# An expert's first product computed transposed, in a fused mixture-of-experts and FFN kernel

## The reference

```
tid = clip(token_ids, 0, 24999);  e = min(tid // 6250, 3)
g = silu(xn @ M.T);  u = xn @ M.T;  y = (g * u) @ M.T      # einsum 'bsd,fd', M = ctx[e]
x = x + tanh(g_xattn) * y
h2 = layernorm(x)
f = silu(h2 @ Wg * gate_scale) * (h2 @ Wu * up_scale)      # weights rounded to fp8, 512 -> 1536
x = x + tanh(g_ffn) * (f @ Wd) * down_scale                # 1536 -> 512
```

## Time and profile before

| | |
|---|---|
| median of 3 runs | 424.04 us (422.85 to 427.6) |
| the profiled execution's own time | 427.73 us |
| its span | 426.0 us |
| PE busy, and matmuls | 395.8 us (93%), x2010 |
| DVE, ACT, POOL busy | 234.5, 183.2, 168.9 us |
| steps 0 to 18, from the first Z matmul to the end of Z of step 18 | 23.0 to 156.7 us |

### The profile page before, as it was taken

How to read it: one execution, slowest core, us unless ns; L and a number is a source line. 1 busy time by engine, 2 the same in 40 slices (tenths; PEclk the granted TensorE clock), 3 DMA queues, 4 the chain that set the end, 5 groups by cost and what they waited for, 6 DMA issues and landing times.

```text
span 426.0 us, 6383 instructions
## 1 busy us (share of the span) xinstructions
PE 395.8 (93%) x2010; PEld 197.9 (46%) x2010; DVE 234.5 (55%) x503; ACT 183.2 (43%) x298; POOL 168.9 (40%) x190
## 2 busy tenths in 40 slices
PE   3959799999999999899999999999999999999991
PEld 2625445555555555444444444444444444444440
DVE  5676778988988678477642422224322225222244
ACT  4484547677786654865352222222222222222220
POOL 2437167764586658799630800001700002600003
PEclk9997989999999999999999999999999999999996
DMA  7575212211113101222000100000200000200002
GB/s 277 160 257 151 72 27 76 74 32 46 49 52 75 49 28 51 74 79 93 2 2 2 74 26 0 0 2 0 98 0 0 0 0 0 100 0 0 2 1 98
DMA packets 10508, 22.66 MB, mean 53 GB/s; under 512 B 1624, under 2 KB 1648, under 8 KB 10480
## 3 DMA queue, kind: packets, MB, share of 16 engines
q1 hardware_dynamic: 7920, 13.92, 10.5%
q0 software_dynamic: 2560, 8.39, 6.0%
HBM read 18.11 MB, written 4.19 MB: 52 GB/s over the span
## 4 chain that ended last, share of the span: by engine, by line
PE 84%; DVE 6%; POOL 4%; issue 2%; DMA 1%; ACT 1%; DVEq 0%; POOLq 0%; ACTq 0%
PE bank L1281 35%; PE bank L1194 24%; PE bank L1289 17%; PE bank L1126 5%; POOL w_sum L470 2%; POOL W L473 2%; PE bank L1148 1%; DVE Ml L794 1%; PE bank L1180 1%; DMA xs<-in_x,order 1%; DVE row_hot L777 1%; DVE w_big L836 1%; DVE xs L1107 1%; DMA ws<-in_L_ffn_down_w 1%; DVE X L1104 1%
## 5 line engine op out<-in xcount | busy, mean ns | idle before, releaser
L1281 PE MATMUL bank<-X,W 128*128 128x512 f16 (+1 forms) x768 | 173.5, 379 | 1.0 <-DVE late_norms L1046 1.0
L1281 PEld LDWEIGHTS bank<-X,W 128*128 128x128 bf16 x768 | 74.9, 98 | 92.0 <-DVE late_norms L1046 2.5
L1057 DVE SCALAR_TENSOR_TENSOR cs<-bank,up_mul,cs 128x512 f32<-128x512 f32 x48 | 36.0, 749 | 107.7 <-PE bank L1281 106.2
L1289 PE MATMUL bank<-W,cs 128*128 128x512 bf16 x376 | 88.7, 379 | 1.6 <-DVE X L856 1.6
L645 ACT ACTIVATE cs<-bank,gate_mul 128x512 f32<-128x512 f32 x48 | 32.9, 685 | 76.6 <-PE bank L1281 76.6
L506 POOL TENSOR_TENSOR xs<-xs,X 128x512 f32<-128x512 f32 x12 | 15.3, 1272 | 121.3 <-DVE X L1104 121.0
L652 ACT ACTIVATE cs<-cs 128x512 f16<-128x512 f32 x47 | 29.5, 628 | 76.0 <-DVE cs L1057 76.0
L1194 PE MATMUL bank<-Mh,X 128*128 x152 | 51.4, 401 | 8.6 <-DVE Ml L794 6.1
L1289 PEld LDWEIGHTS bank<-W,cs 128*128 128x128 f16 x376 | 36.5, 98 | 45.2 <-issue 1.8
L1065 DVE TENSOR_TENSOR cs<-cs 128x512 f16<-128x512 f32 x47 | 35.3, 751 | 37.1 <-ACT cs L652 36.0
L470 POOL TENSOR_TENSOR w_sum<-ws,w_big 128x512 f32<-128x512 f32 x36 | 47.3, 1313 | 5.1 <-DVE w_big L836 2.7
(11 more groups left out here) (145 smaller groups left out, 413.8 us busy)
## 6 DMA issues: line engine op xcount, KB each, us to landing
ws<-in_L_ffn_gate_w SPq DMA_DIRECT2D x12, 256.0 KB, 2.8
ws<-in_L_ffn_up_w SPq DMA_DIRECT2D x12, 256.0 KB, 2.6
ws<-in_L_ffn_down_w SPq DMA_DIRECT2D x12, 256.0 KB, 2.5
cs<-in_ctx SPq DMA_DIRECT2D x2, 1024.0 KB, 6.5
X<-in_ctx SPq DMA_DIRECT2D x2, 1024.0 KB, 7.0
xs<-in_x,order POOLq DMA_INDIRECT x16, 3.6
dsc<-in_L_ffn_down_scale SPq DMA_DIRECT2D x1, 256.0 KB, 7.3
out<-xs,order POOLq DMA_INDIRECT x16, 2.8
```

The lines of the kernel that those rows point to most:

```text
L1057: v.scalar_tensor_tensor(out=fuse[:, c % 2, :], in0=UP[c % 2][:], scalar=up_mul[:, c:c + 1], in1=sg[:, c % 2, :], op0=ALU.mult, op1=ALU.mu ...
L1281: ins = t_.matmul(dst[c % 2][:].rearrange("p (t i) -> p t i", t=TPG), w, x2_group(g, part, k), start=(k == 0 and part == 0), stop=(k == KC ...
L1289: ins = t_.matmul(ACC[t][:], fuse_part(g, c, part)[:, t * P:(t + 1) * P], W8[:, down_slab(c), :], start=(c == 0 and part == 0), stop=(c == ...
```

## The change

Z is computed transposed. For each of four column blocks f of the matrix, and each of four k, a 128 x 128 block of the matrix stands still and the 128 columns of the x tile stream: 48 matmuls of 128 x 128 in place of 12 of 128 x 512. Z then comes out with h's index on the partitions, so h needs no transposes: `turn_h`, bank `HT` and `hT_done` go, and `hTh`, `hTl` are made from `h` in SBUF. The scales of a step, picked by a register before, are read from step 4 on at a fixed column of three small tables, which VectorE fills once at the end of step 3.

```diff
-                    act.wait_ge(hT_done, s)
+                    act.wait_ge(h_done, s)
...
-                    a.activation(hTh[:], HT[:], ACT.Copy).then_inc(hhi_done, 1)
+                    a.activation(hTh[:], h[:], ACT.Copy).then_inc(hhi_done, 1)
...
-                if lo >= 1:
-                    act.wait_ge(h_done, s)
-                a.activation(silu_z[:], Z[:], ACT.Silu, scale=z_scale[:, ds(e, 1)]).then_inc(silu_done, 1)
+                if lo >= BY_REGISTER:
+                    act.wait_ge(tables_done, 1)
+                    scale = z_step[:, s:s + 1]
+                else:
+                    scale = z_scale[:, ds(expert_of(words, s), 1)]
+                a.activation(silu_z[:], Z[:], ACT.Silu, scale=scale).then_inc(silu_done, 1)
...
-                v.tensor_tensor(hTl[:], HT[:], hTh[:], ALU.subtract).then_inc(hlo_done, 1)
+                v.tensor_tensor(hTl[:], h[:], hTh[:], ALU.subtract).then_inc(hlo_done, 1)
...
+            def step_tables():
+
+                later = slice(BY_REGISTER, STEPS)
+                n = STEPS - BY_REGISTER
+                v.tensor_tensor(step_hot[:, :, later], e_of[:, later].unsqueeze(1).to_broadcast([P, E, n]),
+                                iota_q[:, 0:E].unsqueeze(2).to_broadcast([P, E, n]),
+                                ALU.is_equal).then_inc(step_hot_done, 1)
...
+                for i, scales in enumerate((z_scale, h_scale, y_scale)):
+                    ins = v.tensor_tensor(step_sel[:, i, :, later], step_hot[:, :, later],
+                                          scales[:].unsqueeze(2).to_broadcast([P, E, n]), ALU.mult)
...
+                v.tensor_tensor(y_step[:, later], mask[:, later], y_all[:, later], ALU.mult).then_inc(tables_done, 1)
...
                 if lo >= 1:
-                    dve.wait_ge(hT_done, s)
-                v.scalar_tensor_tensor(out=h[:], in0=Z[:], scalar=h_scale[:, ds(e, 1)], in1=silu_z[:],
+                    dve.wait_ge(hlo_done, s)
+                scale = h_step[:, s:s + 1] if lo >= BY_REGISTER else h_scale[:, ds(e, 1)]
+                v.scalar_tensor_tensor(out=h[:], in0=Z[:], scalar=scale, in1=silu_z[:],
...
+                if lo == BY_REGISTER - 1:
+                    step_tables()
...
-            def turn_h(s):
-                pe.wait_ge(h_done, s + 1)
-                transpose4(HT, h, hT_done)
+            def expert_block(part, e, k, cols):
+
+                return part[:, ds(e, 1), k, cols].rearrange("p a n -> p (a n)")
+
+            def product_z(e, tile):
+
+                for f in range(KC):
+                    cols = slice(f * P, (f + 1) * P)
+                    for k in range(KC):
+                        for part, half in ((Mh, 0), (Mh, 1), (Ml, 0)):
+                            ins = t_.matmul(Z[:, cols], expert_block(part, e, k, cols), x_tile(tile, half, k),
+                                            start=(k == 0 and half == 0 and part is Mh),
+                                            stop=(k == KC - 1 and part is Ml))
+                ins.then_inc(z_done, 1)
...
                 if lo >= 1:
-                    if lo >= 2:
-                        pe.wait_ge(hlo_done, s - 1)
-                    turn_h(s - 1)
+                    pe.wait_ge(h_done, s)
                 pe.wait_ge(xlo_done, min(s + 1, TILES))
                 pe.wait_ge(mlo_done, KC * (min(lo, E - 1) + 1))
-                product(Z, e, lambda k: x_tile(tile, 0, k), lambda k: x_tile(tile, 1, k), z_done)
+                product_z(e, tile)
```

More of the change, by code:

```diff
@@ L55, in build @@
     WORDS = -(-STEPS // PER_WORD)
+    BY_REGISTER = 4
     assert E == EXPERTS and KC == 4 and D == 512 and IC == 3 * KC and STEPS == 19
@@ L74, in build @@
         xs = sb("xs", [P, TILES, D], F32)
-        Mh = sb("Mh", [P, E * KC * 512], F16)
-        Ml = sb("Ml", [P, E * KC * 512], F16)
+        Mh = sb("Mh", [P, E, KC, 512], F16)
+        Ml = sb("Ml", [P, E, KC, 512], F16)
         X2 = sb("X2", [P, TILES, 2, KC, P], F16)
@@ L136, in build @@
         y_step = sb("y_step", [P, STEPS], F32)
+        z_step = sb("z_step", [P, STEPS], F32)
+        h_step = sb("h_step", [P, STEPS], F32)
+        y_all = sb("y_all", [P, STEPS], F32)
+        step_hot = sb("step_hot", [P, E, STEPS], F32)
+        step_sel = sb("step_sel", [P, 3, E, STEPS], F32)
         pos = sb("pos", [P, STEPS], F32)
@@ L230, in build @@
         y_step_done = sem("y_step_done")
+        step_hot_done = sem("step_hot_done")
+        step_sel_done = sem("step_sel_done")
+        y_all_done = sem("y_all_done")
+        tables_done = sem("tables_done")
         xn_done = sem("xn_done")
@@ L237, in build @@
         h_done = sem("h_done")
-        hT_done = sem("hT_done")
         hhi_done = sem("hhi_done")
@@ L531, in expert_high @@
                     act.wait_ge(mT_done, KC * e + k + 1)
-                    a.activation(Mh[:, (e * KC + k) * 512:(e * KC + k + 1) * 512], banks[k % len(banks)][:],
+                    a.activation(Mh[:, e, k, :], banks[k % len(banks)][:],
                                  ACT.Identity, scale=m_scale[:, e:e + 1]).then_inc(mhi_done, 1)
@@ L619, in step @@
                     expert_high(1, range(2, KC), MT_SECOND)
-                    for i in range(1, WORDS):
-                        load_word(act, words, i)
                 if 1 <= lo < E - 1:
@@ L634, in last_h_high @@
             def last_h_high():
-                act.wait_ge(hT_done, STEPS)
+                act.wait_ge(h_done, STEPS)
                 act.wait_ge(y_done, STEPS - 1)
-                a.activation(hTh[:], HT[:], ACT.Copy).then_inc(hhi_done, 1)
+                a.activation(hTh[:], h[:], ACT.Copy).then_inc(hhi_done, 1)
             def gate_silu(g, c):
@@ L791, in expert_low @@
                 for k in chunks:
-                    w = slice((e * KC + k) * 512, (e * KC + k + 1) * 512)
                     dve.wait_ge(mhi_done, KC * e + k + 1)
-                    v.scalar_tensor_tensor(out=Ml[:, w], in0=banks[k % len(banks)][:], scalar=m_scale[:, e:e + 1],
-                                           in1=Mh[:, w], op0=ALU.mult, op1=ALU.subtract).then_inc(mlo_done, 1)
+                    v.scalar_tensor_tensor(out=Ml[:, e, k, :], in0=banks[k % len(banks)][:], scalar=m_scale[:, e:e + 1],
+                                           in1=Mh[:, e, k, :], op0=ALU.mult, op1=ALU.subtract).then_inc(mlo_done, 1)
             def step_no(ins):
@@ L903, in add_expert @@
             def add_expert(s):
-                dve.wait_ge(y_step_done, s + 1)
+                if s < BY_REGISTER:
+                    dve.wait_ge(y_step_done, s + 1)
+                else:
+                    dve.wait_ge(tables_done, 1)
                 dve.wait_ge(y_done, s + 1)
@@ L910, in add_expert @@
                                        op0=ALU.mult, op1=ALU.add).then_inc(x1_done, 1)
+            def step_tables():
[4 more added lines that the diff above has]
+                                ALU.is_equal).then_inc(step_hot_done, 1)
+                dve.wait_ge(ys_done, E)
+                dve.wait_ge(step_hot_done, 1)
+                for i, scales in enumerate((z_scale, h_scale, y_scale)):
+                    ins = v.tensor_tensor(step_sel[:, i, :, later], step_hot[:, :, later],
+                                          scales[:].unsqueeze(2).to_broadcast([P, E, n]), ALU.mult)
+                ins.then_inc(step_sel_done, 1)
+                dve.wait_ge(step_sel_done, 1)
+                v.tensor_reduce(y_all[:, later], step_sel[:, 2, :, later].rearrange("p e s -> p s e"), AX.X,
+                                ALU.add).then_inc(y_all_done, 1)
+                v.tensor_reduce(z_step[:, later], step_sel[:, 0, :, later].rearrange("p e s -> p s e"), AX.X, ALU.add)
+                v.tensor_reduce(h_step[:, later], step_sel[:, 1, :, later].rearrange("p e s -> p s e"), AX.X, ALU.add)
+                dve.wait_ge(mask_done, 1)
+                dve.wait_ge(y_all_done, 1)
+                v.tensor_tensor(y_step[:, later], mask[:, later], y_all[:, later], ALU.mult).then_inc(tables_done, 1)
             fcount, nread = [0], [0]
@@ L1009, in step @@
                     x1_low(s + 1)
-                step_y_scale(s, e)
+                if lo < BY_REGISTER:
+                    step_y_scale(s, e)
                 if lo + 1 < E:
@@ L1211, in product_y @@
                     pe.wait_ge(x1_done, s)
-                product(Y, e, lambda k: hTh[:, k * P:(k + 1) * P], lambda k: hTl[:, k * P:(k + 1) * P], y_done)
+                n = 0
+                for k in range(KC):
+                    for part, half in ((Mh, hTh), (Ml, hTh), (Mh, hTl)):
+                        ins = t_.matmul(Y[:], half[:, k * P:(k + 1) * P], expert_block(part, e, k, slice(0, 512)),
+                                        start=(n == 0), stop=(n == 3 * KC - 1))
+                        n += 1
+                ins.then_inc(y_done, 1)
             def step(s, lo):
@@ L1303, in down @@
                 ins.then_inc(down_done, 1)
-            pe.wait_ge(hlo_done, STEPS - 1)
```

(1 more changed line is left out.)

1 line of the change is left out of this document (removed).

## The result

| | before | after |
|---|---|---|
| median of the runs compared | 425.09 us (4 runs) | 454.48 us (454.14 to 456.19, 4 runs) |
| the profiled execution | 427.73 us | 454.41 us |
| its span | 426.0 us | 452.7 us |
| PE busy, matmuls | 395.8 us, x2010 | 414.5 us, x2618 |

A forecast was written before the change was run, and what follows sets the result against it. TensorE bounds the steps, and in the new Z its sequencer's register instructions, 5.6 us against 2.6 of array work. Steps +19.1, start +3.7 and end -0.4 give +22.4 us on the 424.04 median: 446.4 us, range 436 to 456.

The forecast's parts named there:

- The steps, +19.1: From Z of step 3 to Z of step 18: 98.4 us become 117.4, the sequencer setting Z.
- Release: Ordinary step: the square ends and the sequencer is free for Z's register work 2.3 us after the previous Z's end.
- h decides, at 1.65: Step 3 has no square, so h frees the sequencer 1.65 us after Z's end; the period is 7.25 us.
- Z's length in the chain: Sign that the forecast is right: Z 4.6 to 5.2 us long, its matmul starts 0.09 to 0.13 us apart.
- A, the array sets Z: Rival: register work costs little or runs ahead; a step is 6.2 us, total 417 to 421; chance 7%.
- B, exposed weight loads: Rival: weight loads not hidden at 128 columns; Z 4.0 us, +0.95 a step, total 440 with the start; chance 6%.
- C, the sequencer runs ahead of a waiting matmul: Rival: it works ahead through Y; 7.0 us a step, total 433 with the start; chance 6%.
- D, the clock falls in the steps: Rival: half clock makes steps some 3 us longer, up to 490; a few stretches give 455 to 465; chance 7%.
- The end, -0.4: End of the steps: the transposes of h behind Y 17 go, saving 0.4 us.
- The tables, at nothing: Eight small VectorE operations, under 3 us once, during Z of step 4, so they cost nothing.
- The start, +3.7: Steps 0 to 3 start from a standstill: step 0 +1.5, step 1 0, step 2 +2.0, step 3 +0.2 us.
- step 1: 0: Z of step 1, at the half clock already, takes 0.85 + 5.30 us; the sequencer's 5.6 adds nothing.

The follow-up runs named there:

- from_four: The changed kernel with Z transposed only from step 4; steps 0 to 3 do Z as 12 matmuls and turn h as before: 443.69 us, ratio 1.0469.
- before_regs: The kernel before with three unused register instructions added ahead of each matmul of Z but the first: 463.17 us, ratio 1.0932.
- z_fixed: The changed kernel with Z's expert and tile written in as constants, so Z has no register instructions: 430.73 us, ratio 1.015.
- grouped: The changed kernel with Z's address arithmetic grouped into fewer, fused instructions, all still behind the norms: 442.67 us, ratio 1.0414.
- early_split: The changed kernel with grouped address arithmetic, the tile's and first block's placed ahead of the previous step's norms wait: 432.55 us, ratio 1.0202.
- mixed: Steps 0 to 3 as in the kernel before, from step 4 Z transposed with grouped and early addresses, no tables: 421.01 us, ratio 0.9953.

## Why the prediction was right, and where it was not

**In all.** The measured 454.48 us are 8.1 above the forecast and lie inside its range by 1.5. The range had been set for the price of register work, exposed loads and the clock, not for the start, so that it covered the start's miss is in part luck.

**The steps, +19.1 forecast: held.** Z of step 3 to Z of step 18 took 118.0 us (65.73 to 183.76), forecast 117.4. `from_four`, where nothing else is changed, gives 19.8 us by medians, with the end's -0.4 in it. The pieces of the ordinary step held one by one. Release at Z's end + 2.4 (98.55 to 100.9), forecast 2.3. From there to the end of Z 5.4 us, forecast 5.6. Middle periods 7.7 to 7.9, forecast 7.9; with two squares 8.3, forecast 8.4; the last ones 7.3, forecast 7.4. The price of a register instruction, 0.105 us from seven of them, measured 0.097 in `before_regs`. That the sum is right to 0.6 us owes something to chance: two periods were 1.9 us longer than forecast, and the others together 1.3 shorter. One of the two shows a step of the prediction that failed. From step 3 to 4 "h decides, at 1.65" was wrong; the sequencer came free at 68.4, 2.7 behind Z's end, when the low part of the next x had been made behind h:

```profile
67.63 0.68 DVE L864 SCALAR_TENSOR_TENSOR X<-bank,X 128x512 f16<-128x512 f32 x1
```

Of the signs, Z's length in the chain was named as 4.6 to 5.2 us and is 4.2 (step 8), with starts 0.086 us apart on average. The prediction's own terms give 4.35: the sequencer comes free 2.3 behind Z's end and the array comes to Z at 3.55, so 1.25 of the 5.6 us have passed by then. The sign was worked out wrongly, not the sum.

**The rivals.** A, the array sets Z: out by the result, and `z_fixed` shows what it would have been, 6.25 a step (forecast 6.2). B, exposed weight loads: out by the same 2.70 us. C, the sequencer runs ahead of a waiting matmul: out by `grouped` against `early_split`, 6.7 against 6.25 us. D, the clock falls in the steps: the granted clock is 1.00 from 66 to 184 us; it had a part in the start only (0.67 and 0.68 in Z of steps 2 and 3).

**The end, -0.4: held** (268.9 against 269.3 us).

**The tables, at nothing: nearly held, and only for this kernel.** Their eight operations took 2.1 us on VectorE, under the 3 forecast, though one of them took 0.83 where 0.43 had been the most. The period from step 5 to 6 was 8.9 us against 7.9 forecast, with VectorE behind, and 8.0 without the tables. The prediction named their cover, Z of step 4, and in `early_split`, where that Z is short, they are open: the period from Z 4 to Z 5 was 10.3 us, in `mixed` without them 6.1.

**The start, +3.7: this term was too small.** In the two profiled executions it is +7.4 (65.73 against 58.35), by medians about 10.8. Between the profiled executions (450.1 forecast, 454.41 measured) that is 3.7 of the 4.3 us missed. Two things were missed. First, some 4 us of late completions in step 1: TensorE's semaphores for Y of step 0 and the last transposes came 4 us after the ends that its records model (44.78 for 40.46, 46.21 for 42.11), which delays `Mh`, `Ml` and Z of step 2. No row of the kernel before shows such a thing, and the step priced as "step 1: 0" took no account of it.

Second, I set the sum against one profiled execution and moved it to the median as it was. That execution had Z of step 3 at the half clock, 4.42 us; in `from_four` the same 12 matmuls took 2.76. So against a run with the full clock there step 3 lost 2 to 3 us, not 0.2 (from Z of step 2 to Z of step 3: 12.54 us, 9.88 in `from_four`, 11.69 in the kernel before). "The difference does not sit in the steps as far as the rows show" was wrong: a part of it sat in a row that I quoted. The trace shows this of one execution of the kernel before. That its others had the full clock there is inferred, from their mean granted clocks: with 0.988 or 0.989 the spans were 421.1 to 421.7 us but for one of 422.9, with 0.980 they were 424.3, 425.8 and 426.0. The clock does not explain all of it, since with 0.986 they lie between 422.4 and 424.8.

**Open.** What makes the completions late. The runs show two conditions, gathers under way and many TensorE instructions at the same time, and no mechanism. The Trainium skill (NOTIFIC — the notification-queue block, Overflow: three behaviours, one of which stalls the engine) says that the block which writes an engine's trace records to memory always holds back inside itself rather than lose one, so that it can stall an engine. That would fit both conditions. It would also mean that part of the start's loss belongs to being profiled; every execution here was profiled, so no run tells.

## What to carry to other kernels

On an engine whose operands are addressed by registers, count the sequencer's instructions per loop body and price them by the distance between their starts behind a standstill, not by the length of their records; cutting a matmul into smaller ones multiplies them while the array's time stays. If they are the limit, put address arithmetic in one block so that operations are fused, and ahead of the next instruction that waits. Before moving a sum from one profiled execution to the median, look for a stretch at the half clock in that execution.

## What the hardware showed beyond that

- **A fused register instruction** with up to six operations takes some 0.13 us from start to start (four of them at 108.341 to 108.739 in `grouped`), a single one 0.097:

```profile
L1242 PEldq FUSED_REGOPS  x4: 74/74/74, 108.3 to 108.7; - x4
```

- **VectorE beside GpSimd.** In `early_split` the three `step_sel` operations above are the same size and took 1.31, 0.21 and 1.28 us. The long ones began while GpSimd was at a slab operation, and ended within 0.1 us of it:

```profile
67.46 1.27 POOL L480 TENSOR_TENSOR w_sum<-ws,w_big 128x512 f32<-128x512 f32 x1
68.80 1.26 POOL L483 TENSOR_TENSOR W<-w_sum,w_big 128x512 bf16<-128x512 f32 x1
```

- **A chain that names an unknown queue** on a kernel of one core: compare the start of the waiting instruction with the matmul records. Their ends are modelled, and here they ran up to 4.3 us ahead of the semaphores.
